# Three PSUM banks for the scores and one for the row-maximum scores, instead of two and two, in an attention and feed-forward layer

## The chip, the cores and the metric

The kernel runs on one core of one Trainium2 chip. Its metric is the device time of one launch in microseconds (us), the median of three runs: 2845.18 us before the change (2844.33 to 2846.65). The engines are named as in the profile: PE is TensorE's matmul side and PEld its loading of weights, DVE is VectorE, ACT is ScalarE, POOL is GpSimd, SP is SyncE, which here only issues DMAs. Matmuls write into PSUM, of which the kernel uses all eight banks of 512 float32 values for each of 128 partitions.

## The reference

A pre-norm layer on 16 sequences of 512 tokens and 256 channels, all float32:

```
x = x + attention(layernorm(x))      # 32 query heads over 16 key/value heads, head size 64
x = x + ffn(layernorm(x))            # rank-64 factors: U1, V1, gelu, U2, V2
scores = q @ k.T / 8 + alibi_slope * (key_pos - query_pos)   # causal, -inf above the diagonal
attn = softmax(scores);  out = (attn @ v) @ W_out
```

## The kernel before

**Splitting.** Float32 factors are split into a high and a low float16 part, and every product is the sum of three float16 matmuls. So most values pass through three engines: ACT rounds the high part out of a PSUM bank (`copy`, L677), DVE computes the low part (`low`, L836), SP moves both to the partitions at which the matmuls read them. For the softmax the order is ACT `exp` from a scores bank into `p_f` (L718), ACT `p_hi` (L677), POOL `p_lo` (L1082).

**Batches, steps, segments.** One loop iteration is one batch element `i`; it has 16 steps `s`, one for each key/value head (two query heads), and each step has 5 segments `n`. The stages run pipelined over the steps: the row maxima of head pair g stand in step g + 2, its scores and exponentials in step g + 7 (`ATT`), the product with v in the step after. With 16 batches there are 16 x 16 x 5 = 1280 blocks of scores and as many blocks of row-maximum scores. The code is written out in full for all iterations, and each engine has its own instruction stream, in the order of the code; engines wait for each other by semaphores that count finished blocks.

**Two kinds of scores.** `scores(s, n)` computes the transposed score block, keys on partitions, with the maximum already subtracted through extra rows of the operands, and ACT exponentiates it. To know the maximum beforehand, `max_scores(s, n)` computes the plain scores first (queries on partitions) and `maxima(s, n)` on DVE adds the causal mask in place in the bank and reduces it to one column (L909: one custom instruction and one reading of the accumulator for each tile; a segment has one tile of 512 columns or two of 384 + 128 or 256 + 256). After every four steps the maxima are transposed (`transpose_max`), split by ACT and DVE, and written by DMA into the query operand (`neg_max_t` to `q_hi_aug`, L388), for which PE waits at the scores of the first of the next four heads.

**PE's order within a segment** (L635 to L669): `scores(s, n)`, in some segments a feed-forward matmul or the transposition, `max_scores(s, n)`, then what the segment has of projections (k at n = 0 of odd steps, q at n = 1 of even and n = 2 of odd steps, the output projection at n = 4, v at n = 4), the attention product `attend` at n = 1 and n = 3, and the feed-forward parts. So in an even step `max_scores(s, 0)` and `max_scores(s, 1)` have only `scores(s, 1)` between them, and `max_scores(s, 2)` and `max_scores(s, 3)` only `scores(s, 3)`. In an odd step a projection stands in the first of these gaps and the q projection in the second.

**DVE's order** (L932 to L1051): in a segment first the normalised rows of the second layernorm and the low part of the transposed maxima, if due, then `maxima(s, n)`, then the low parts of v, k, q and x, the output sum (`x_acc`), and at n = 1 and n = 3 `normalise` (`rden`, `o_f`), which waits for `attend`.

**Banks and their waits.** Two banks in turn hold `scores`, two `max_scores`, one `o_acc`, three the projections and everything else. PE may write scores block b when ACT has exponentiated block b - 2, and max block b when DVE has reduced block b - 2:

```
if SEG * a + n - 1 > 0:
    pe.wait_ge(exp_done, at(SEG * a + n - 1))
bank = score_bank[(SEG * s + n) % 2]
```

Of the kernel before, what the change touches and what calls it, by code (L numbers as in the profile page):

```python
# [26 lines left out]
ACT = mybir.ActivationFunctionType  # L27
# [14 lines left out]
SEG = 5  # L42
# [51 lines left out]
def q_segment(s):  # L94

    return 2 if s % 2 else 1
# [16 lines left out]
def projection_order():  # L113

    uses = []
    for s in range(KV):
        for n in range(SEG):
            if (s, n) in H_PAIRS:
                uses += [("h", 2 * H_PAIRS[s, n]), ("h", 2 * H_PAIRS[s, n] + 1)]
            if n == MAX_SEG and s % 4 == 2:  # L120
                uses.append(("max", s))
            if (s, n) in X_PAIRS:
                uses.append(("x", X_PAIRS[s, n]))
            if n == K_SEG and s % 2 == 1:
                uses.append(("k", s))
            if n == OUT_SEG:
                uses.append(("out", s))
            if (s, n) in LN2_T_AT:
                uses.append(("ln2", LN2_T_AT[s, n]))
            if n == q_segment(s):  # L130
                uses.append(("q", s))
            if n == V_SEG and s % 8 < 4:
                uses.append(("v", s))
            if (s, n) in U1_AT:
                uses.append(("p", U1_AT[s, n]))
            if (s, n) == Y_AT:
                uses += [("y", 0), ("y", 1)]
            if (s, n) in U2_PAIRS:
                uses.append(("u", U2_PAIRS[s, n]))
    return uses  # L140

BANKS = 3
PROJ = {use: k % BANKS for k, use in enumerate(projection_order())}


# [61 lines left out]
def layer(nc, x, w_qkv, w_out, u1, v1, b1, u2, v2, b2, k_aug, q_aug, ident_d, ident_b_d, causal_d, out):  # L209
    B = x.shape[0]  # L210
    ctx = ExitStack()
    with ctx:
        def sb(name, shape, dt):
            return ctx.enter_context(nc.sbuf_tensor(name, shape, dt))

        def psum(name):
            return ctx.enter_context(nc.psum_tensor(name, [P, 512], F32))

        def sem(name):
            return ctx.enter_context(nc.semaphore(name))  # L220
# [23 lines left out]
        p_f = sb("p_f32", [P, 3, 512], F32)  # L244
# [29 lines left out]
        h_lo = sb("h_lo", [P, 2, S], F16)  # L274
        qf_hi, qf_lo = h_hi[:, 0, :], h_lo[:, 0, :]

        score_bank = [psum("scores0"), psum("scores1")]
        max_bank = [psum("max_scores0"), psum("max_scores1")]
        o_bank = psum("o_acc")
        proj_bank = [psum(f"proj{b}") for b in range(BANKS)]  # L280

# [17 lines left out]
        exp_done, hi_p, lo_p = sem("exp_done"), sem("hi_p"), sem("lo_p")  # L299
# [13 lines left out]
        block = ctx.enter_context(nc.Block())  # L313

        def at(count):

            if not isinstance(count, Count):
                return count
            if not count.regs:
                return count.value()  # L320
            if not count.plus:
                return count.regs[count.times]
            count.regs["eng"].reg_add(count.regs["target"], count.regs[count.times], count.plus)
            return count.regs["target"]

        def max_place(s, n):

            return max_bank[(SEG * s + n) % 2], 2

        def iterations(name, eng, body):  # L330
            body(Count(0), FIRST)
# [5 lines left out]
        def ffn_batch(i, s):  # L337

            return i - 1 if s >= 8 else i - 2
# [105 lines left out]
        def _(pe):  # L445
# [5 lines left out]
            def mm(out_ap, lhs, rhs, start, stop):  # L451
                return nc.tensor.matmul(out_ap, lhs, rhs, start=start, stop=stop, skip_group_check=True)  # L452
# [9 lines left out]
            def transpose_x(b, pair):  # L462

                bank = proj_bank[PROJ["x", pair]]
                if pair == 0:
                    pe.wait_ge(xn_done, at(T * (b + 1)))
                for c in range(DC):
                    for t in range(2):
                        col = (c * 2 + t) * P
                        last = nc.tensor.transpose(bank[:, col:col + P], xt[:, 2 * pair + t, c * P:(c + 1) * P], ident[:, :])  # L470
                last.then_inc(pe_ln1, 1)

            transpose_x(0, 0)
            transpose_x(0, 1)
            proj_free = {PROJ["x", pair]: (lo_ln1, pair + 1) for pair in range(2)}
            pe.wait_ge(split_done, 3)

            def body(i, mode):

                def next_proj(use, semaphore, count):  # L480

                    b = PROJ[use]
                    if b in proj_free:
# [5 lines left out]
                def scores(s, n):  # L489
                    a = i * KV + s - ATT  # L490
                    r = (s - ATT) % RING
                    if n == 0:
                        if (s - ATT) % 4 == 0:
                            q4 = (s - ATT) // 4
                            pe.wait_ge(m_in[q4 % 2], at(32 * (2 * i + q4 // 2 + 1)))

                    if SEG * a + n - 1 > 0:
                        pe.wait_ge(exp_done, at(SEG * a + n - 1))
                    bank = score_bank[(SEG * s + n) % 2]
                    for h, kt, off, width in SCORE_BLOCKS[n]:  # L500
                        keys = slice(kt * P, (kt + 1) * P)
                        o = bank[:, off:off + width]
                        mm(o, ka[:, r, keys], qa[:, r, h, kt * P:S], True, False)

                        mm(o[:, 0:P], causal[:, S - P:S], ident_b[:, :], False, False)
                        last = mm(o, kb[:, r, keys], qb[:, r, h, kt * P:S], False, True)
                    last.then_inc(pe_scores, 1)

                def max_scores(s, n):
                    g = i * KV + s - 2  # L510
                    r = (s - 2) % RING
                    if n == 0:
                        use = 2 * i + (s - 2) // RING + 1
                        pe.wait_ge(qdup_in[r], at(QK_DMAS * 16 * use))
                        if s % 2 == 0:
                            pe.wait_ge(kdup_in[r // 2], at(QK_DMAS * 16 * use))
                            pe.wait_ge(kaug_in[r // 2], at(16 * use))
                    bank, back = max_place(s, n)
                    if SEG * g + n + 1 - back > 0:
                        pe.wait_ge(max_done, at(SEG * g + n + 1 - back))  # L520
                    for h, qt, off in MAX_BLOCKS[n]:
                        width = (qt + 1) * P
                        last = mm(bank[:, off:off + width], qb[0:MAX0, r, h, qt * P:(qt + 1) * P],
                                  kb[0:MAX0, r, 0:width], True, True)
                    last.then_inc(pe_max, 1)
# [100 lines left out]
                for s in steps(mode):  # L626
# [8 lines left out]
                    for n in range(SEG):  # L635
                        if in_stage(mode, s, ATT):
                            scores(s, n)
# [37 lines left out]
        def _(act):  # L675
            def copy(out_ap, in_ap, scale=1.0):
                return nc.scalar.activation(out_ap, in_ap, ACT.Copy, scale=scale)  # L677
# [6 lines left out]
            def high_x(b, pair):  # L684
                act.wait_ge(pe_ln1, at(2 * b + pair + 1))
                copy(xnt[0][:, :, pair * 256:(pair + 1) * 256],
                     proj_bank[PROJ["x", pair]][:, :].rearrange("p (c q) -> p c q", c=DC)).then_inc(hi_ln1, 1)

# [16 lines left out]
            def body(i, mode):  # L705
                def proj(*use):
                    return proj_bank[PROJ[use]]

                def exponentiate(s, n):
                    count = SEG * (i * KV + s - ATT) + n  # L710
                    act.wait_ge(pe_scores, at(count + 1))


                    back = 2 if s == 0 and n < 2 else 3
                    if count - back + 1 > 0:
                        act.wait_ge(lo_p, at(count - back + 1))
                    k = SEG * s + n
                    nc.scalar.activation(p_f[:, k % 3, :], score_bank[k % 2][:, :], ACT.Exp).then_inc(exp_done, 1)  # L718

                def high_p(s, n):  # L720
                    a = i * KV + s - ATT
# [23 lines left out]
                for s in steps(mode):  # L745
# [3 lines left out]
                    for n in range(SEG):  # L749
# [5 lines left out]
                        if n == 0 and in_stage(mode, s, ATT + 1):  # L755
                            if s > 0:
                                high_p(s - 1, SEG - 1)
                            else:
                                a = i * KV - ATT - 1
                                act.wait_ge(exp_done, at(SEG * (a + 1)))  # L760
                                copy(p_hi[:, 1, SEG - 1, :], p_f[:, (SEG * KV - 1) % 3, :]).then_inc(hi_p, 1)
                        if in_stage(mode, s, ATT):
                            exponentiate(s, n)
# [8 lines left out]
                        if n == O_SEG and in_stage(mode, s, ATT + 1):  # L772
                            a, slot = g - ATT - 1, s % 2
# [28 lines left out]
                        if ffn_in(i, s):  # L802
                            f = ffn_batch(i, s)
# [29 lines left out]
        def _(dve):  # L833
            def low(out_ap, bank, high, scale):

                return nc.vector.scalar_tensor_tensor(out=out_ap, in0=bank, scalar=scale, in1=high,  # L836
                                                      op0=ALU.mult, op1=ALU.subtract)
# [46 lines left out]
            def low_x(b, pair):  # L884
                dve.wait_ge(hi_ln1, at(2 * b + pair + 1))
                cols = slice(pair * 256, (pair + 1) * 256)
                low(xnt[1][:, :, cols], proj_bank[PROJ["x", pair]][:, :].rearrange("p (c q) -> p c q", c=DC),
                    xnt[0][:, :, cols], 1.0).then_inc(lo_ln1, 1)
# [286 lines left out]
```

## Time and profile before

| | |
|---|---|
| median of three runs | 2845.18 us |
| the profiled execution | 2847.87 us, of which 2846.1 us span |
| PE busy | 2688.1 us, 94% |
| ACT busy | 2178.4 us, 77% |
| POOL busy | 2000.1 us, 70% |
| DVE busy | 1990.9 us, 70% |
| granted TensorE clock, mean | 0.988 |

The span is what lies between the first and the last instruction. One batch takes some 178 us. A wait in the profile is idle time of one engine just before an instruction, put down to what released it. PE and PEld are two sides of one engine: one stop of it often shows on both, so their waits are not added.

### The profile page before, as it was taken

How to read it: one execution, taken by the hardware profiler on the slowest of the kernel's cores; microseconds unless marked ns; L12 is line 12 of the kernel's file. 1: busy time of each engine (PE TensorE's matmuls, PEld its weight loads, DVE VectorE, ACT ScalarE, POOL GpSimd, SP SyncE). 2: the span in 40 equal slices, each digit the busy share in tenths (PEclk: the TensorE clock that was granted, in tenths of full speed). 3: DMA queues.
4: the chain of work that ended last, by engine and by line, in shares of the span. 5: the costliest groups of instructions: out<-in, count | busy, mean ns of one | idle time of the engine just before them, and what ended most of it. 6: DMA issues, size and time to landing. Idle time of an engine off the chain costs nothing.

```text
span 2846.1 us, 83739 instructions
## 1 busy us (share of the span) xinstructions
PE 2688.1 (94%) x31112; PEld 1835.5 (64%) x31112; DVE 1990.9 (70%) x6795; ACT 2178.4 (77%) x3892; POOL 2000.1 (70%) x1816
## 2 busy tenths in 40 slices
PE   4999999999999999999999999999999999999985
PEld 1566666666666666666666666666666666666662
DVE  6667677676766767677676777767667676777743
ACT  3777878778777887878878787787878878787782
POOL 1667777777777777777777777777767777777773
PEclk9999999999999999999999999999999999999996
DMA  6444345344444444444444445434444454445421
GB/s 169 91 97 91 87 99 93 87 96 93 95 88 96 89 91 95 87 99 96 88 95 92 94 88 101 91 87 97 89 95 94 94 87 91 96 88 101 88 45 26
DMA packets 495147, 260.83 MB, mean 92 GB/s; under 512 B 317962, under 2 KB 493066, under 8 KB 494474
## 3 DMA queue, kind: packets, MB, share of 16 engines
q1 hardware_dynamic: 494740, 255.47, 42.8%
q8 instruction: 247, 4.05, 0.6%
q14 instruction: 160, 1.31, 0.1%
HBM read 27.73 MB, written 8.39 MB: 13 GB/s over the span
## 4 chain that ended last, share of the span: by engine, by line
PE 65%; ACT 11%; issue 7%; POOL 5%; DMA 5%; SPq 4%; DVE 3%; ACTq 0%; POOLq 0%; DVEq 0%
PE proj L452 31%; PE scores L452 16%; PE o_acc L452 10%; PE max_scores L452 7%; POOL p_lo L1082 3%; ACT p_hi L677 3%; ACT p_f L718 3%; DMA o_t<-o_hi_lo 2%; ACT L718 2%; DMA q_hi_aug<-neg_max_t_lo 2%; ACT h_f L809 2%; POOL h_lo L1112 1%; POOL o_hi_lo L1094 1%; SPq L422 1%; DVE max_scores L909 1%
## 5 line engine op out<-in xcount | busy, mean ns | idle before, releaser
L1082 POOL TENSOR_TENSOR p_lo<-p_f,p_hi 128x512 f16<-128x512 f32 x1280 | 1481.5, 1169 | 778.7 <-ACT p_hi L677 777.8
L909 DVE CUSTOM_DVE_ANT_0 max_scores<-max_scores,causal 128x512 f32<-128x512 f32 (+3 forms) x2048 | 970.0, 507 | 313.7 <-PE max_scores L452 299.6
L718 ACT ACTIVATE p_f<-scores 128x512 f32<-128x512 f32 x1280 | 755.7, 590 | 169.0 <-PE scores L452 143.2
L677 ACT ACTIVATE p_hi<-p_f 128x512 f16<-128x512 f32 x1280 | 800.0, 625 | 14.2
L452 PE MATMUL scores<-q_hi_lo,k_lo_hi 128*128 128x512 f16 (+3 forms) x2048 | 614.4, 300 | 34.5 <-ACT p_f L718 18.3
L452 PE MATMUL scores<-q_hi_aug,k_hi_aug 128*128 128x512 f16 (+3 forms) x2048 | 586.1, 299 | 0.0
L452 PE MATMUL o_acc<-v_hi_one,p_lo 128*128 128x65 f16 x5120 | 517.2, 194 | 8.8 <-POOL p_lo L1082 7.8
L452 PE MATMUL max_scores<-k_hi_aug,q_hi_aug 96*128 96x512 f16 (+3 forms) x2048 | 489.8, 300 | 29.0 <-issue 17.5
L452 PE MATMUL o_acc<-v_hi_one,p_hi 128*128 128x65 f16 x5120 | 517.0, 194 | 0.0
L452 PE MATMUL o_acc<-v_lo,p_hi 128*128 128x64 f16 x5120 | 516.4, 193 | 0.0
L452 PEld LDWEIGHTS o_acc<-v_hi_one,p_lo 128*128 128x128 f16 x5120 | 471.2, 98 | 41.5 <-POOL p_lo L1082 22.8
L452 PEld LDWEIGHTS o_acc<-v_lo,p_hi 128*128 128x128 f16 x5120 | 468.1, 98 | 38.5
L452 PEld LDWEIGHTS o_acc<-v_hi_one,p_hi 128*128 128x128 f16 x5120 | 467.4, 97 | 0.0
L452 PE MATMUL scores<-ident_bf,causal 128*128 128x128 bf16 x2048 | 448.1, 219 | 0.0
L452 PE MATMUL proj<-wo_hi,o_t 128*128 128x256 f16 x2048 | 382.2, 275 | 13.7 <-DMA o_t<-o_hi_lo 13.6
L452 PE MATMUL proj<-xn_t_hi,wqkv_lo 128*128 128x512 f16 x768 | 293.6, 382 | 28.8 <-DVE x_acc L916 16.4
L1094 POOL TENSOR_TENSOR o_hi_lo<-o_f,o_hi_lo 128x512 f16<-128x512 f32 x256 | 296.3, 1157 | 3.4 <-ACT o_hi_lo L677 3.4
L452 PE MATMUL proj<-xn_t_hi,wqkv_hi 128*128 128x512 f16 x768 | 293.1, 382 | 0.0
L452 PE MATMUL proj<-xn_t_lo,wqkv_hi 128*128 128x512 f16 x768 | 293.0, 381 | 0.0
L909 DVE DVE_READ_ACCUMULATOR2_ANT row_max<- 128x1 f32 x2048 | 284.2, 139 | 1.3
L452 PE MATMUL proj<-wo_lo,o_t 128*128 128x256 f16 x1024 | 280.8, 274 | 0.0
L452 PEld LDWEIGHTS scores<-q_hi_lo,k_lo_hi 128*128 128x128 f16 x2048 | 199.6, 97 | 114.3 <-ACT p_f L718 24.8
(107 smaller groups left out, 4282.4 us busy)
## 6 DMA issues: line engine op xcount, KB each, us to landing
q_hi_aug<-q_pair_hi SPq DMA_DIRECT2D x512, 64.0 KB, 2.0
q_hi_lo<-q_pair_hi SPq DMA_DIRECT2D x512, 64.0 KB, 2.0
q_hi_lo<-q_pair_lo SPq DMA_DIRECT2D x512, 64.0 KB, 2.0
k_hi_aug<-k_pair_hi SPq DMA_DIRECT2D x256, 64.0 KB, 2.0
k_lo_hi<-k_pair_hi SPq DMA_DIRECT2D x256, 64.0 KB, 2.0
k_lo_hi<-k_pair_lo SPq DMA_DIRECT2D x256, 64.0 KB, 2.0
x_rows<-in_L_attn_inputs SPq DMA_DIRECT2D x17, 512.0 KB, 4.5
x_acc<-in_L_attn_inputs SPq DMA_DIRECT2D x64, 128.0 KB, 2.5
```

What stands on the lines that cost most here:

```text
L422: sp.dma_start_transpose(ot[:, kv % OUT_RING, :, :].rearrange("p a (t q) -> p (a t) q", q=P), o_hl[:, slot, :, :].rearrange("p a q -> p (a ...
L452: return nc.tensor.matmul(out_ap, lhs, rhs, start=start, stop=stop, skip_group_check=True)
L677: return nc.scalar.activation(out_ap, in_ap, ACT.Copy, scale=scale)
L718: nc.scalar.activation(p_f[:, k % 3, :], score_bank[k % 2][:, :], ACT.Exp).then_inc(exp_done, 1)
L809: nc.scalar.activation(h_f[:, c % 2, :], proj("h", c)[:, :], ACT.Gelu_apprx_tanh, bias=b1c[:, c:c + 1], scale=1.0 / FFN_SCALE).then_inc(ge ...
L909: last = nc.vector.tensor_tensor_reduce(out=bank, in0=bank, in1=causal[:, (T - 1 - qt) * P:S], scale=1.0, scalar=-3e38, op0=ALU.add, op1=A ...
L1082: nc.gpsimd.tensor_tensor(p_lo[:, slot, n, :], p_f[:, k % 3, :], p_hi[:, slot, n, :], ALU.subtract).then_inc(lo_p, 1)
L1094: nc.gpsimd.tensor_tensor(o_hl[:, slot, 1, :], o_f[:, slot, :, :].rearrange("p t c -> p (t c)"), o_hl[:, slot, 0, :], ALU.subtract).then_i ...
L1112: nc.gpsimd.tensor_tensor(h_lo[:, c % 2, :], h_f[:, c % 2, :], h_hi[:, c % 2, :], ALU.subtract).then_inc(lo_h, 1)
```

## The change

`scores` gets a third bank and `max_scores` keeps one, so that eight banks remain in use. PE may now write scores block b when ACT has exponentiated block b - 3, and max block b when DVE has reduced block b - 1. Nothing else is edited.

```diff
 BANKS = 3
+SCORE_BANKS = 3
 PROJ = {use: k % BANKS for k, use in enumerate(projection_order())}
...
-        score_bank = [psum("scores0"), psum("scores1")]
-        max_bank = [psum("max_scores0"), psum("max_scores1")]
+        score_bank = [psum(f"scores{b}") for b in range(SCORE_BANKS)]
+        max_bank = psum("max_scores")
...
         def max_place(s, n):
 
-            return max_bank[(SEG * s + n) % 2], 2
+            return max_bank, 1
...
-                    if SEG * a + n - 1 > 0:
-                        pe.wait_ge(exp_done, at(SEG * a + n - 1))
-                    bank = score_bank[(SEG * s + n) % 2]
+                    block = (SEG * a + n).value()
+                    if block - SCORE_BANKS + 1 > 0:
+                        pe.wait_ge(exp_done, block - SCORE_BANKS + 1)
+                    bank = score_bank[block % SCORE_BANKS]
...
-                    nc.scalar.activation(p_f[:, k % 3, :], score_bank[k % 2][:, :], ACT.Exp).then_inc(exp_done, 1)
+                    nc.scalar.activation(p_f[:, k % 3, :], score_bank[count.value() % SCORE_BANKS][:, :], ACT.Exp).then_inc(exp_done, 1)
```

Both programs have the same instructions in the same order on every engine; bank names and the counts that PE waits for differ. PE, segments 0 and 1 of an even step, before:

```order
9300 L452 MATMUL scores0<-q_hi_lo,k_lo_hi 128x512 [waits exp_done]
9301 L452 MATMUL scores0<-ident_bf16,causal 128x128
9302 L452 MATMUL scores0<-q_hi_aug,k_hi_aug 128x512
9303 L452 MATMUL max_scores0<-k_hi_aug,q_hi_aug 128x512 [waits kaug_in2,max_done,kdup_in2,qdup_in4]
9304 L452 MATMUL scores1<-q_hi_lo,k_lo_hi 128x512 [waits exp_done]
9305 L452 MATMUL scores1<-ident_bf16,causal 128x128
9306 L452 MATMUL scores1<-q_hi_aug,k_hi_aug 128x512
9307 L452 MATMUL max_scores1<-k_hi_aug,q_hi_aug 128x384 [waits max_done]
9308 L452 MATMUL max_scores1<-k_hi_aug,q_hi_aug 128x128
```

The same place of PE in the changed kernel:

```order
9300 L453 MATMUL scores2<-q_hi_lo,k_lo_hi 128x512 [waits exp_done]
9301 L453 MATMUL scores2<-ident_bf16,causal 128x128
9302 L453 MATMUL scores2<-q_hi_aug,k_hi_aug 128x512
9303 L453 MATMUL max_scores<-k_hi_aug,q_hi_aug 128x512 [waits kaug_in2,max_done,kdup_in2,qdup_in4]
9304 L453 MATMUL scores0<-q_hi_lo,k_lo_hi 128x512 [waits exp_done]
9305 L453 MATMUL scores0<-ident_bf16,causal 128x128
9306 L453 MATMUL scores0<-q_hi_aug,k_hi_aug 128x512
9307 L453 MATMUL max_scores<-k_hi_aug,q_hi_aug 128x384 [waits max_done]
9308 L453 MATMUL max_scores<-k_hi_aug,q_hi_aug 128x128
```

Nothing moved. Row 9307 waited for the maxima of the block before 9303 and now waits for those of 9303 itself, which stands four matmuls ahead of it; row 9304 waits for an exponential that lies one block further back.

## Rows read from the trace of the kernel before

**Rows 1.** The page, section 1: busy time of each engine.
```profile
PE 2688.1 (94%) x31112; PEld 1835.5 (64%) x31112; DVE 1990.9 (70%) x6795; ACT 2178.4 (77%) x3892; POOL 2000.1 (70%) x1816
```

**Rows 2.** Waits of PEld: engine, line, releaser: total us, times, longest us.
```profile
PEld scores L452 <- ACT p_f L718: 24.8, 52, 2.7
PEld scores L452 <- DMA q_hi_aug<-neg_max_t_lo: 24.7, 26, 1.9
PEld o_acc L452 <- POOL p_lo L1082: 22.8, 51, 2.2
PEld proj L452 <- DVE k_pair_lo L836: 20.1, 64, 2.3
PEld max_scores L452 <- DVE row_max L909: 16.9, 25, 1.8
```

**Rows 3.** Timeline, PEld, step 14: start us, us, ..., loads for max blocks 0, 1, 3.
```profile
990.87 0.10 PEld L452 LDWEIGHTS max_scores<-k_hi_aug,q_hi_aug 96*128 96x128 f16 x1
991.58 0.10 PEld L452 LDWEIGHTS max_scores<-k_hi_aug,q_hi_aug 96*128 96x128 f16 x1
...
995.92 0.10 PEld L452 LDWEIGHTS max_scores<-k_hi_aug,q_hi_aug 96*128 96x128 f16 x1
```

**Rows 4.** Timeline, PE: matmuls of max block 1, in step 14 and in step 0.
```profile
991.79 0.38 PE L452 MATMUL max_scores<-k_hi_aug,q_hi_aug 96*128 96x384 f16 x2
...
842.62 0.39 PE L452 MATMUL max_scores<-k_hi_aug,q_hi_aug 96*128 96x384 f16 x2
```

**Rows 5.** Timeline, DVE, step 14: maxima of block 0, then around block 2.
```profile
991.64 0.70 DVE L909 CUSTOM_DVE_ANT_0 max_scores<-max_scores,causal 128x512 f32<-128x512 f32 x1 [0.38 <-issue]
992.26 0.14 DVE L909 DVE_READ_ACCUMULATOR2_ANT row_max<- 128x1 f32 x1
...
996.08 0.28 DVE L836 SCALAR_TENSOR_TENSOR neg_max_t_lo<-proj,neg_max_t_hi 32x128 f16<-32x128 f32 x1 [0.61 <-ACT neg_max_t_hi L677]
996.28 0.41 DVE L909 CUSTOM_DVE_ANT_0 max_scores<-max_scores,causal 128x256 f32<-128x256 f32 x1
...
997.01 0.13 DVE L909 DVE_READ_ACCUMULATOR2_ANT row_max<- 128x1 f32 x1
```

**Rows 6.** Timeline, PEld, step 4: loads for max blocks 0, 1, 3.
```profile
889.00 0.10 PEld L452 LDWEIGHTS max_scores<-k_hi_aug,q_hi_aug 96*128 96x128 f16 x1
...
889.71 0.31 PEld L452 LDWEIGHTS max_scores<-k_hi_aug,q_hi_aug 96*128 96x128 f16 x2
...
893.60 0.10 PEld L452 LDWEIGHTS max_scores<-k_hi_aug,q_hi_aug 96*128 96x128 f16 x1
```

**Rows 7.** Timeline, DVE, step 4: before and in block 0, then block 2's last reading.
```profile
889.56 0.69 DVE L836 SCALAR_TENSOR_TENSOR v_lo<-proj,v_hi_one 128x512 f16<-128x512 f32 x1 [1.73 <-ACT v_hi_one L677]
890.17 0.41 DVE L916 SCALAR_TENSOR_TENSOR x_acc<-proj,x_acc 128x256 f32<-128x256 f32 x1
...
891.10 0.14 DVE L909 DVE_READ_ACCUMULATOR2_ANT row_max<- 128x1 f32 x1
...
894.19 0.14 DVE L909 DVE_READ_ACCUMULATOR2_ANT row_max<- 128x1 f32 x1
```

**Rows 8.** Step 0: PEld's two stops; DVE's last readings before block 0 and in it.
```profile
842.62 0.11 PEld L452 LDWEIGHTS max_scores<-k_hi_aug,q_hi_aug 96*128 96x128 f16 x2 [0.47 <-DVE row_max L909]
844.17 0.10 PEld L452 LDWEIGHTS proj<-xn_t_hi,wqkv_lo 128*128 128x128 f16 x1 [1.44 <-DVE xn_t_lo L836]
...
842.42 0.14 DVE L909 DVE_READ_ACCUMULATOR2_ANT row_max<- 128x1 f32 x1
...
844.57 0.14 DVE L909 DVE_READ_ACCUMULATOR2_ANT row_max<- 128x1 f32 x1
```

**Rows 9.** Step 11: PEld's load for max block 3, DVE's end of block 2.
```profile
965.33 0.10 PEld L452 LDWEIGHTS max_scores<-k_hi_aug,q_hi_aug 96*128 96x128 f16 x1
...
965.95 0.14 DVE L909 DVE_READ_ACCUMULATOR2_ANT row_max<- 128x1 f32 x1
```

**Rows 10.** The tile `max_scores`: all its weight loads, first and last start.
```profile
L452 PEld LDWEIGHTS max_scores<-k_hi_aug,q_hi_aug x2048: 95/98/152, 44.4 to 2734.5; 96*128 96x128 f16 x187
```

**Rows 11.** Stretches: length, busy of PE, PEld, DVE, ACT, POOL, granted clock, DMA, GB/s.
```profile
1178.00:2600.00 1422.00, 1385.16 (x16216) 953.89 (x16213) 1020.67 (x3522) 1133.22 (x2030) 1038.88 (x943) 1.00 0.44 92
...
2730.00:2740.00 10.00, 6.59 (x102) 5.15 (x100) 4.38 (x17) 9.37 (x16) 7.92 (x8) 1.00 0.15 29
```

## The prediction

> **What bounds the kernel now.** I read the busy times first: PE has 94%, the next engine 77% [rows 1], and in the long steady stretch PE is busy for 1385 of 1422 us [rows 11]. PE works through its list in order, so a stop of PE anywhere, once the pipeline is full, is time added to the end unless a later stop that is there already shrinks by it. Then the waits of PEld, where PE's stops begin [rows 2]. The two that the change touches are small: 24.8 us behind ACT's exponential, 16.9 us behind DVE's maxima. The third view is the timeline of PE and DVE around the max blocks [rows 3 to 9]. It decides, because the change swaps two distances: PE may run three scores blocks ahead of ACT instead of two, and one max block ahead of DVE instead of two, so that writing a max block and reading it no longer overlap at all.
>
> **What the third scores bank removes.** The wait for `p_f` [rows 2], at most 24.8 us. With the block three back to wait for, which ACT has done a whole segment earlier, I expect all 52 stops to go, and then PE comes earlier to the next max block, where part is lost again. I take 20 us; the ends are 0 and 24.8.
>
> **What the single max bank adds.** PE's new rule: the matmuls of max block b start when DVE's last accumulator reading of block b - 1 has ended, plus the signal. The signal can be read where PE waited for just that: DVE's reading ended at 842.42 + 0.14 = 842.56, the load came at 842.62 [rows 8], so 0.06 us, and the matmul began with it [rows 4]. Where PE does not wait, a matmul can start up to 0.21 us after its load (991.58 and 991.79) [rows 3, 4], as the array is still busy. So I count delays by the matmuls: load start plus 0.21 at n = 1, plus 0.06 at n = 3, where the matmul ahead is narrow.
>
> Even steps, n = 1 (only one scores block between the two max blocks). Step 14: DVE ends block 0 at 992.26 + 0.14 = 992.40 [rows 5], PE could start at 992.46 and had started at 991.79 [rows 4]: 0.67 us. DVE began that block only 0.77 us after PE's load of it (990.87 to 991.64) and works 0.76 us, so the loop of PE, DVE and back is 1.59 us, where the loads are 0.71 us apart; a stop of PE before it shifts all of it and shortens nothing. I take 0.70 us for the five steps 6 to 14. In steps 2 and 4 DVE comes to the block later, behind `v_lo`, which waited for ACT and through it for PE's own v projection, and `x_acc`: end 891.10 + 0.14, start possible at 891.30, was 889.71 + 0.21 = 889.92: 1.38 us [rows 6, 7].
>
> Even steps, n = 3. Step 4: block 2 ends at 894.33, so 894.39 against 893.66: 0.73 [rows 6, 7]; I take 0.75 for steps 0, 4, 8, 12, since DVE has the h of the second layernorm in front in one of them. In steps 2, 6, 10, 14 DVE waits for ACT's transposed maxima before block 2 and ends at 997.14: 997.20 against 995.98, 1.22 us [rows 3, 5].
>
> Step 0 has two stops already, and what counts is when the q projection starts: 844.17 before [rows 8]. After, max block 1 can start at 844.57 + 0.14 + 0.06 = 844.77 and its two matmuls take 0.39 us to their modelled end [rows 4], of which the next overlaps the larger part: I take 0.22, so 844.99: 0.8 us more.
>
> Odd steps are mostly free, since a projection stands between. The exceptions are step 11 at n = 3, behind a long `h_f` on DVE: 965.95 + 0.14 + 0.06 = 966.15 against 965.39, 0.76 us [rows 9]; and step 5, where the feed-forward end crowds DVE in the same manner (estimate 0.8), and small ones, estimated from the same pattern at 0.8 together.
>
> Per batch: 5 x 0.70 + 2 x 1.38 + 4 x 0.75 + 4 x 1.22 + 0.8 + 2.4 = 3.5 + 2.8 + 3.0 + 4.9 + 0.8 + 2.4 = 17.4 us. Sixteen batches: 278 us.
>
> **What of it is hidden.** A stop hides in a later stop of PE whose releaser was started before the first. (1) PE waits for the DMA of the transposed maxima, 24.7 us [rows 2]. Its chain starts at n = 2 of steps 6, 10, 14, 2, ahead of the 1.22 us stop at n = 3, and the wait follows at the next step's n = 0. 24.7 / 26 = 0.95 us, mostly below 1.22: I take 16 of the 24.7. (2) PE waits for `p_lo`, 22.8 us: the last exponential lies before n = 1 of the step, so the n = 1 stop lies partly in between: half, 11 us. (3) PE waits for `k_pair_lo`, 20.1 us: in odd steps, right behind its own projection, which shifts with PE: 0. (4) The maxima wait, 16.9 us, mostly at step 0, is inside the 0.8 there. The ends are 0 and the whole of (1) to (3), 67.6 us.
>
> **Sum.** 278 - 20 - 16 - 11 = 231 us on the profiled execution's 2847.9 us: 3079 us. That execution is 2.7 us above the median of the runs, so 3076 us. ACT, POOL and DVE have room for nothing worse: their busy shares fall to some 71, 65 and 65%, and they are waited for less than before.
>
> **Rivals.**
> 1. *PE's other waits swallow more.* All of the removable and hidden ones go in full: 278 - 24.8 - 67.6 = 186 us, 3031 us after the 2.7. For it: ACT and POOL get 8% more time for the same work. Against: the k wait hangs on PE itself.
> 2. *DVE never catches up.* The price of a stop above assumes that DVE works off its backlog while PE stands, so that the second stop of a step is not larger for the first. If every late finish counts in full: of the 1280 blocks (the first and last of their 2048 loads at 44.4 and 2734.5 [rows 10]) I find 433 whose load started before DVE had ended the block ahead, 390 us in sum and 416 us with the signal. 416 - 25 = 391 us, 3236 us. Against: in step 14 DVE idled 0.38 us before block 0 [rows 5], so it starts each even step without backlog, and a stop counted by its load is 0.15 us too long at n = 1.
> 3. *The clock.* The new stops, about 16 in a batch, take PE from 97% to some 90% busy. If TensorE's granted clock fell from 1.00 to a mean of 0.95, 5% of PE's 2688 us come on top, 134 us: 3210 us. Against: in 2730 to 2740 us PE was busy for 6.6 of 10 us with stops like these and was granted 1.00 [rows 11].
> 4. *Not slower.* The waits do not bind, because DVE's reading fits between the blocks, and only the third scores bank shows: 2847.9 - 24.8 = 2823 us, 2820 after the 2.7. It decides at n = 1 of the even steps: DVE would have to end 0.06 us before 991.79. It works 0.76 us by itself, from 991.64 on, which is longer than the whole 0.71 us between the loads. Nothing in the trace speaks for it but the small total of the present wait (16.9 us), which says only that two blocks of distance were enough.
>
> The Trainium skill bears on rival 3: its page "TensorE: Matmul & The Clock Gate", section "A second HAM failure mode: psum-queue depth-cycling", tells of a kernel whose matmul groups of 512 columns cycled through PSUM banks with short idle times between them, and whose clock swung between the two levels. By that rule this change, which makes just such pauses, would end at rival 3's time or above. The row at 2730 us disagrees, and it stands at 4%.
>
> **Chances.** Forecast (3040 to 3130) 0.70; rival 1 (3000 to 3040) 0.15; rival 2 (above 3130) 0.09; rival 3 0.04; rival 4 0.02. The likeliest is 3076 us. The range for 8 in 10 is 3015 to 3145. What a measurement can tell from no change is about 0.2%, 5.7 us; only rival 4 leads to faster (0.01) or the same (0.01), slower has 0.98.
>
> **What would show it.** In the changed profile PEld's wait for `row_max` rises from 16.9 to some 250 to 300 us with about 300 stops, at n = 1 and n = 3 of even steps. A stop's next load comes 0.06 us after DVE's reading. The wait for `p_f` is gone. The wait for the maxima's DMA shrinks to less than half. The granted clock stays at 0.98 or more. PE's busy time hardly moves, its share falls to 87%. I am wrong if the stops stand elsewhere, or if their sum is right and the time is not because other waits grew: ACT's exponential behind POOL, or `o_acc` behind `p_lo`.

## The result, and the profile after

The changed kernel takes 3095.5 us, the median of four runs (3093.2 to 3096.3), against 2845.9 us, the median of four runs of the kernel before: a ratio of 1.0875, 95% interval 1.0856 to 1.0894. It is 250 us slower. Forecast were 3076 us and 3015 to 3145. The profiled execution took 3095.6 us.

The page after: busy time of the engines (section 1), which answers to [rows 1]. PE has the same matmuls and 89% of the span instead of 94%; DVE, ACT and POOL have lost share as well. So nothing became a bottleneck by its work, and PE stands still more: its idle time grew by 197 us and its busy time, which was to stay as it was with a share of 87%, by 51 us.

```profile
PE 2738.7 (89%) x31112; PEld 1838.0 (59%) x31112; DVE 2059.5 (67%) x6795; ACT 2178.3 (70%) x3892; POOL 2006.3 (65%) x1816
```

PEld's waits after, as in [rows 2] (a line number is one or two higher where the new lines shift it):

```profile
PEld max_scores L453 <- DVE row_max L911: 324.2, 301, 3.2
PEld proj L453 <- issue: 60.2, 136, 9.7
PEld max_scores L453 <- issue: 57.6, 64, 2.5
PEld proj L453 <- DVE k_pair_lo L838: 18.9, 64, 2.1
...
PEld o_acc L453 <- POOL p_lo L1084: 12.2, 9, 3.4
...
PEld scores L453 <- ACT p_f L720: 1.8, 2, 1.0
...
PEld scores L453 <- DMA q_hi_aug<-neg_max_t_lo: 0.7, 3, 0.3
```

Read against [rows 2]: the wait for DVE's maxima went from 16.9 us in 25 stops to 324.2 us in 301; the wait for the exponential, from 24.8 to 1.8; for the maxima's DMA, from 24.7 to 0.7; for `p_lo`, from 22.8 to 12.2; for `k_pair_lo` it stayed (20.1 and 18.9). A wait of PEld is up to 0.2 us longer than what the matmuls lose, so 324 us of waits are not 324 us of time. The row for the maxima also leaves some out: of the 64 stops put down to `issue`, 30, with 30.6 us, stand before block 0 of a step and end 0.12 us after DVE's last reading of the block before, so they are waits for the maxima too. PE has a further semaphore instruction there, since block 0 also waits for the DMAs of q and k, and the profile names no releaser for them.

The timeline after, PEld and then DVE, step 14 of one batch: start us, duration us, instruction, and in brackets the idle time before it and its releaser. It is the place of [rows 3, 5].

```profile
1084.18 0.10 PEld L453 LDWEIGHTS max_scores<-k_hi_aug,q_hi_aug 96*128 96x128 f16 x1 [0.69 <-issue]
...
1085.58 0.11 PEld L453 LDWEIGHTS max_scores<-k_hi_aug,q_hi_aug 96*128 96x128 f16 x2 [0.83 <-DVE row_max L911]
...
1090.65 0.10 PEld L453 LDWEIGHTS max_scores<-k_hi_aug,q_hi_aug 96*128 96x128 f16 x1 [1.22 <-DVE row_max L911]
```

```profile
1083.93 0.14 DVE L911 DVE_READ_ACCUMULATOR2_ANT row_max<- 128x1 f32 x1
...
1084.77 0.70 DVE L911 CUSTOM_DVE_ANT_0 max_scores<-max_scores,causal 128x512 f32<-128x512 f32 x1 [0.42 <-issue]
1085.38 0.14 DVE L911 DVE_READ_ACCUMULATOR2_ANT row_max<- 128x1 f32 x1
...
1090.46 0.13 DVE L911 DVE_READ_ACCUMULATOR2_ANT row_max<- 128x1 f32 x1
```

PE and DVE take turns. DVE's reading of block 0 ends at 1085.52 and PE's load of block 1 comes at 1085.58; the reading of block 2 ends at 1090.59 and the load of block 3 comes at 1090.65. Both are the 0.06 us forecast, and the second stop, 1.22 us, is the number of the prediction. The first load here shows something new: block 0 itself waited 0.69 us. It is one of the 30 stops without a releaser: DVE's last reading of the block before, block 4 of step 13, ends at 1084.07, and the load comes at 1084.18.

Step 4 after, the place of [rows 6, 7], PEld and then DVE:

```profile
974.27 0.11 PEld L453 LDWEIGHTS max_scores<-k_hi_aug,q_hi_aug 96*128 96x128 f16 x2 [1.55 <-DVE row_max L911]
```

```profile
972.53 0.69 DVE L838 SCALAR_TENSOR_TENSOR v_lo<-proj,v_hi_one 128x512 f16<-128x512 f32 x1 [1.25 <-ACT v_hi_one L679]
973.14 0.41 DVE L918 SCALAR_TENSOR_TENSOR x_acc<-proj,x_acc 128x256 f32<-128x256 f32 x1
...
974.07 0.14 DVE L911 DVE_READ_ACCUMULATOR2_ANT row_max<- 128x1 f32 x1
```

`v_lo` and `x_acc` still stand ahead of block 0 on DVE, and PE now waits for the end of that row of work.

Stretches after (length, busy of PE, PEld, DVE, ACT, POOL, granted clock, DMA share, GB/s), which answer to [rows 11]:

```profile
0.00:160.00 160.00, 100.05 (x750) 51.24 (x751) 94.86 (x266) 70.06 (x113) 50.94 (x44) 0.87 0.44 112
...
1000.00:1194.00 194.00, 176.58 (x2055) 120.09 (x2053) 133.85 (x449) 142.10 (x256) 131.25 (x120) 1.00 0.42 87
1194.00:2800.00 1606.00, 1460.89 (x16826) 989.58 (x16825) 1098.51 (x3661) 1172.68 (x2104) 1079.27 (x980) 1.00 0.41 85
```

PE is busy for 91% of the steady stretch, at a granted clock that rounds to 1.00.

### The profile page after: what moved, and what is told of

The parts are those of the page before. It is cut to its first block and busy times, and to the rows that moved or that the text cites. A ratio compares the mean times of both kernels' runs of the same rounds, so it can differ in the third digit from the quotient of the medians.

```text
span 3093.8 us, 83739 instructions
## 1 busy us (share of the span) xinstructions
PE 2738.7 (89%) x31112; PEld 1838.0 (59%) x31112; DVE 2059.5 (67%) x6795; ACT 2178.3 (70%) x3892; POOL 2006.3 (65%) x1816
## 3 DMA queue, kind: packets, MB, share of 16 engines
q14 instruction: 160, 1.31, 0.1%
## 5 line engine op out<-in xcount | busy, mean ns | idle before, releaser
L453 PE MATMUL max_scores<-k_hi_aug,q_hi_aug 96*128 96x512 f16 (+3 forms) x2048 | 496.4, 303 | 286.6 <-DVE row_max L911 268.8
L453 PEld LDWEIGHTS o_acc<-v_hi_one,p_lo 128*128 128x128 f16 x5120 | 474.1, 98 | 36.7 <-POOL p_lo L1084 12.2
L453 PEld LDWEIGHTS max_scores<-k_hi_aug,q_hi_aug 96*128 96x128 f16 x2048 | 181.3, 98 | 408.2 <-DVE row_max L911 324.2
L679 ACT ACTIVATE q_pair_hi<-proj 128x512 f16<-128x512 f32 x256 | 152.5, 596 | 248.2 <-PE proj L453 248.2
```

## The experiments

Each ran beside the kernel before, which took 2849.9 to 2851.1 us there. The changed kernel itself was measured beside a kernel before of 2845.9 us; by its ratio of 1.0875 it is set at 3100.5 us in these comparisons. The intervals of two ratios leave such a difference uncertain by some 7 us.

**Without the third scores bank**

```diff
-SCORE_BANKS = 3
+SCORE_BANKS = 2
```

> Two scores banks in turn and one max bank (seven banks in use): the changed kernel without its third scores bank. Theory (the single max bank costs, the third scores bank gives a little back): the stops of PE before the scores in segment 4 of steps 1, 3 and 13 return, 1.33 us per batch by the comparison of the two traces, so 3096 + 21 = 3117 us, within 3108 to 3125. Rival (the third bank is worth nothing once PE waits for maxima, since ACT has caught up during those waits): 3096 us within 5.

Measured: 3105.1 us, ratio 1.0899 (1.0881 to 1.0918), so 4.6 us above the changed kernel's 3100.5; the two profiles' last max blocks lie 10.8 us apart. The intervals overlap. The time lies below the expected range of 3108 to 3125 us, and the rival, within 5 us of the changed kernel, is nearer: the third bank is worth 5 to 11 us, not 21. Its PEld waits for the exponential and for the maxima:

```profile
PEld max_scores L453 <- DVE row_max L911: 323.3, 300, 3.2
...
PEld scores L453 <- ACT p_f L720: 22.5, 45, 2.7
```

The stops before the scores came back as expected, but not in the time. Block by block, the two traces part by 0.49 us at segment 4 of step 1, 0.40 us in step 3 and 0.46 us in step 13, and come together again by 0.47 us at block 0 of step 14. There the changed kernel has the 0.69 us stop seen above. Block 0 of step 14 waits for two things, DVE's maxima of the block before and the DMAs of k's low part. SP had issued two of these (timeline of the changed kernel, SP's issues), the second 0.6 us behind the first, at 1081.56, and such a DMA lands 2.0 us after its issue (the page, section 6: KB each, us to landing):

```profile
1080.93 1.23 SPq L406 DMA_DIRECT2D k_lo_hi<-k_pair_lo  x2
```

```profile
k_lo_hi<-k_pair_lo SPq DMA_DIRECT2D x256, 64.0 KB, 2.0
```

So k was there at 1083.56, 0.6 us before the load, and it was DVE's reading, which ended at 1084.07, that held PE. Over the batches, 9 of the 16 stops end 0.12 us after DVE's last reading, with k landed 0.1 to 0.8 us before the load; in six the load comes 0.06 us after k's last landing, and for one the trace shows no cause. In the run with two banks stops of both kinds are 0.3 to 0.5 us shorter: the third bank brings PE there some 0.5 us earlier, but not DVE or k. So what the third bank wins in step 13 PE spends at step 14, in most batches waiting for DVE's maxima, else for k. The places, sizes and times are measured; no run removed either wait.

**Only the wait, no shared bank**

```diff
-            return max_bank[(SEG * s + n) % 2], 2
+            return max_bank[(SEG * s + n) % 2], 1
```

> The kernel before with its two banks of each kind in turn, and only the count in the wait of the max blocks tightened: block b waits for the maxima of block b - 1. No bank is shared between a matmul being written and a block being read. Theory (the loss is the wait itself, PE writing and DVE reading in series): the same as the run with two scores banks and one max bank, about 3117 us, within 3 us of that run. Rival (part of the loss is that PE and DVE meet in the same bank, a slower access or restart): clearly below that run, by 10 us or more.

Measured: 3109.7 us, ratio 1.0910 (1.0894 to 1.0926), 4.6 us above the run before, with 324.4 us in 301 waits for DVE's maxima. That is more than the 3 us expected, the intervals overlap, and of the 6 us between the two profiles 3.4 lie at step 0, where the clock fell in six batches instead of four (see the last part). Two banks in turn do not help once the wait is tightened, and the rival, 10 us or more below, is out. The loss is the order in time, PE writes, DVE reads, PE writes; that both use the same PSUM bank costs nothing that shows.

**The q projection between max blocks 0 and 1**

```diff
-                        if in_stage(mode, s, 2):
+                        if in_stage(mode, s, 2) and not (n == 1 and s % 2 == 0):
                             max_scores(s, n)
...
                             project(next_proj(("q", s), lo_q, i * KV + s + 1), s * P, pe_q)
+                        if in_stage(mode, s, 2) and n == 1 and s % 2 == 0:
+                            max_scores(s, n)
```

> The changed kernel, and in even steps max_scores(s, 1) is written after the q projection of its segment instead of ahead of it, which puts 1.3 us of matmuls between max blocks 0 and 1 and takes them from between blocks 1 and 2. Theory (stops come from max blocks that lie closer on PE than the 1.5 to 1.6 us of writing, reading and signalling): the stops of five steps (0.69 us by matmuls) go and those of steps 2 and 4 shrink by 1.2 us, block 2 stays free: 16 x (3.45 + 2.4) = 94 us less, 3002 us, within 2985 to 3025. Rival (DVE is too slow on the whole, and a stop that is avoided at block 1 comes back at block 2 or 3): 3080 to 3100 us, with stops of 0.7 us or more at n = 2.

Measured: 2976.5 us, ratio 1.0444 (1.0428 to 1.0460): 124 us less, where 94 were expected. Waits for the maxima fell to 188.1 us in 210. No stop came back at block 2. I had left out step 0 (1.0 us per batch) and taken too little for steps 2 and 4; with the next stops of steps 10 and 12 (0.18 and 0.36 us less) the two traces part by 121 us in all. The rival, a DVE too slow on the whole, falls: with the same work for DVE half of the loss is gone.

**A shorter reading of block 0**

```diff
-                        bank = max_place(s, n)[0][:, off:off + (qt + 1) * P]
+                        width = 2 * P if n == 0 else (qt + 1) * P
+                        bank = max_place(s, n)[0][:, off + (qt + 1) * P - width:off + (qt + 1) * P]
...
-                            out=bank, in0=bank, in1=causal[:, (T - 1 - qt) * P:S], scale=1.0, scalar=-3e38,
+                            out=bank, in0=bank, in1=causal[:, S - width:S], scale=1.0, scalar=-3e38,
```

> The changed kernel, but DVE takes the maximum of block 0 of every step over its last 256 columns instead of all 512 (that part of the computation is left out), so this reading is shorter by some 0.26 us (0.75 us against 0.49 us for a first tile of 256 columns in the trace), and nothing is moved. Theory (DVE's reading stands on PE's path at n = 1 of the eight even steps, one to one): 8 x 0.26 x 16 = 33 us less, 3063 us, within 3055 to 3070. Rival (the stops are set by when DVE comes to the block, by ACT or by its backlog, and the length of one reading is absorbed): under 10 us less, 3086 to 3096 us.

Measured: 3067.1 us, ratio 1.0762 (1.0746 to 1.0778): 33 us less, as the theory has it, and 29 us less by the two profiles; the intervals do not tell the two apart. Block 1's load comes 0.25 to 0.27 us earlier in seven of the eight even steps, 0.20 in step 8. Two later stops grew, (10, 3) and (12, 3) (step, segment) by 0.23 and 0.25 us, 8 us in sum, since there DVE was held by the second layernorm and not by PE. A microsecond saved on DVE in front of a waiting PE is one on PE, unless the next stop hangs on something that did not move.

**The low part of v behind the maxima**

```diff
-    return 1 if s >= 8 else 0
+    return 1
```

> The changed kernel, and DVE computes the low part of v always after the next step's maxima of block 0 instead of ahead of them, as it does already for the second half of the heads. Theory (in steps 2 and 4 the stop of PE at max block 1 is 1.4 us instead of 0.7 because v_lo and x_acc stand ahead of block 0 on DVE): these two stops shrink by the 0.6 us of v_lo each, 2 x 0.6 x 16 = 19 us less than the changed kernel. Rival (the projection bank that v_lo frees later makes PE wait elsewhere, or the stop is held by x_acc anyway): within 6 us of the changed kernel.

Measured: 3074.7 us, ratio 1.0779 (1.0760 to 1.0798): 26 us less, 19 expected. The waits at block 1 of steps 2 and 4 fell from 1.54 and 1.65 us to 0.88 and 0.89, the size of those of steps 6 to 14, with `x_acc` still ahead of block 0. So their excess was `v_lo`, and not `x_acc`.

**Max block 3 behind the attention product, in addition** (`MAX_AFTER` names the steps' segments whose max block is written later, and behind what)

```diff
+MAX_AFTER = {(0, 1): 'q', (0, 3): 'attend'}      # (s % 2, n)
...
+                def max_at(s, n, place):
+                    if in_stage(mode, s, 2) and MAX_AFTER.get((s % 2, n), "segment") == place:
+                        max_scores(s, n)
...
                             attend(s, n // 2)
+                        max_at(s, n, "attend")
```

> As the run with the q projection ahead of max block 1, and in even steps max block 3 is written after the attention product of its segment (0.92 us more distance from block 2, 0.92 us less to block 4). Theory (each stop is 1.5 to 1.6 us minus the distance on PE): at n = 3 the four plain stops go (0.75 us each) and the four behind the transposed maxima shrink by 0.92, 107 us; at n = 4 steps 6, 8, 10, 12 have only 0.7 us left and get stops of some 0.8 us, 54 us: 53 us less than that run, 2923 us, within 2900 to 2945. Rival (DVE as a whole is late by then, its backlog decides): no gain, 2960 to 2985.

Measured: 2917.1 us, ratio 1.0222 (1.0207 to 1.0238), 60 us below the run with q ahead of block 1; 53 expected. Waits for the maxima fell to 120.6 us. At n = 4 new waits stand where they were expected: 0.86, 0.68, 0.47 and 0.47 us in steps 6, 8, 10 and 12.

**All max blocks spread**

```diff
+MAX_AFTER = {(0, 0): 'scores1', (0, 1): 'q', (0, 3): 'attend', (0, 4): 'out',
+             (1, 0): 'k', (1, 1): 'attend', (1, 2): 'q', (1, 3): 'attend', (1, 4): 'out'}
```

> The changed kernel with the max blocks spread evenly over PE's list: block 0 of even steps after scores block 1, all others at the end of their segment, after the projection, attention product or output projection in it, so that no two stand closer than about 1.5 us. Theory (distance decides): the stops shrink to those at step 0 and behind the transposed maxima and the second layernorm, some 2 us per batch; with the third scores bank this is 2850 to 2885 us. Rival (DVE's other work, q, k, v low parts and the normalisation, now comes too late behind the maxima, and new waits of PE for them replace the old ones): 2900 us or more, with stops of PE before o_acc or the projections.

Measured: 2961.0 us, ratio 1.0377 (1.0362 to 1.0393), where 2850 to 2885 were expected. The rival won: 44 us worse than the run before. PEld's waits in this run, the two longest:

```profile
PEld proj L454 <- DVE k_pair_lo L848: 84.4, 64, 2.3
PEld max_scores L454 <- DVE row_max L921: 77.7, 197, 2.1
```

The waits for the maxima shrank as intended, and the wait for the low part of k grew from 19 to 84 us. DVE works in order with the maxima first in each segment, so a max block that PE writes late holds back `k_pair_lo`, whose bank PE needs for the next projection. With the odd steps as they were, two runs further down, this wait is back at 19.1 us.

**The same order with two and two banks**

> The same spread order with the banks of the kernel before, two for the scores and two for the maxima. Theory (with two max banks DVE had slack enough, so the order is worth nothing by itself): within 10 us of the kernel before. It also says what single bank costs once the blocks are spread: the theory expects under 35 us between this run and the spread run with three and one. Rival (the spread order delays DVE's other results): 20 us or more slower than the kernel before.

Measured: 2921.9 us, ratio 1.0244 (1.0229 to 1.0259), 71 us above the kernel before, where at most 10 were expected: the rival again, and with the same wait:

```profile
PEld proj L453 <- DVE k_pair_lo L846: 85.4, 64, 3.1
```

So most of the loss of the spread order is its own, and the banks add 39 us to it, a little over the 35 that were allowed.

**Spread in the even steps alone**

```diff
+MAX_AFTER = {}
+MAX_AFTER.update({(s, 1): 'q' for s in range(0, 16, 2)})
+MAX_AFTER.update({(s, 3): 'attend' for s in range(0, 16, 2)})
+MAX_AFTER.update({(s, 4): 'out' for s in (6, 8, 10, 12)})
...
-    return 1 if s >= 8 else 0
+    return 1
```

> Three scores banks and one max bank; max block 1 of even steps after the q projection, block 3 of even steps after the attention product, block 4 of steps 6, 8, 10 and 12 after the output projection, v_lo late as in the run with the low part of v; odd steps as in the kernel before, since the fully spread order made PE wait 84 us for the low part of k. Theory (distance on PE against 1.5 to 1.6 us): from the run with max block 3 after the attention product the stops at n = 4 of the four steps go, (0.86 + 0.68 + 0.47 + 0.47) x 16 = 40 us, of which some 6 us come back at block 0 of step 7, and v_lo gives 14 us: 2917 - 48 = 2869 us, within 2855 to 2890. Rival (new waits for other low parts, as in the fully spread order): 2900 us or more.

Measured: 2893.3 us, ratio 1.0158 (1.0140 to 1.0177). By the ratios that is 18 us below the run with block 3 behind the attention product, and 48 were expected: a miss. The waits at n = 4 are gone, and `row_max` is down to 67.3 us, but block 0 of steps 7 and 13 now waits 0.63 and 0.50 us, which stands in the row of `issue`:

```profile
PEld max_scores L457 <- issue: 69.5, 90, 2.2
PEld max_scores L457 <- DVE row_max L924: 67.3, 123, 1.6
```

Of the 69.5 us in the first row, 47.0 us in 58 stops end 0.12 us after DVE's last reading, so they are waits for the maxima as well; in the changed kernel these were 30.6 us. I had counted only step 7 behind its moved block, and not step 13. By the two traces steps 6 to 13 gave 12 us, where 40 less 6 were expected, and `v_lo` gave 4 us for 14, since with block 1 behind the q projection the stops of steps 2 and 4 were already down to 0.40 and 0.50 us. It is the best order found for three and one banks, and it does not reach the kernel before.

**That order with two and one, and with two and two banks**

> The same order, with two scores banks and one max bank. Theory (the third scores bank was worth only 7 us in the changed kernel because the stops before max blocks repay it at steps 14, 2 and 4; with fewer such stops it is worth more): 12 to 25 us slower than the same order with three scores banks. Rival (its worth does not depend on them): 5 to 9 us slower.

> The same order, with two banks of each kind as in the kernel before. Theory (with two max banks the order matters little): within 10 us of the kernel before, and 15 to 30 us faster than the same order with two scores banks and one max bank, since some 100 us of stops before max blocks become about 20 us and other waits of PE take a part of the difference. Rival (the order itself costs): 15 us or more slower than the kernel before.

Measured: 2904.6 us with two and one, ratio 1.0199 (1.0178 to 1.0220), and 2853.6 us with two and two, ratio 1.0017 (1.0008 to 1.0027). The third scores bank is worth 11 us here, just under the 12 to 25 of the theory and above the rival's 9; the intervals of the two ratios touch, so that it is worth more than in the changed kernel stays open. The reason that the theory gave does not hold at step 14: at its block 0 PE still gives back 0.55 us per batch. The order by itself is nearly free, 0.17% slower than the kernel before. The second max bank is worth 51 us even in this order, where 15 to 30 were expected: to bring the blocks apart removed 80% of the loss with two and one banks (255 us, now 51) and not all of it. With three and one banks, the banks of the change, 40 us are left.

## Why the prediction was right

The mechanism was right, place by place, and the time is 20 us above the likeliest value, a miss of 8% of the change. The two traces, compared at the first matmul of each max block and averaged over the batches, give for each of the prediction's terms (us per batch):

| term | predicted | measured |
|---|---|---|
| n = 1, steps 6 to 14 (five) | 3.5 | 3.67 |
| n = 1, steps 2 and 4 | 2.8 | 2.81 |
| n = 3, steps 0, 4, 8, 12 | 3.0 | 3.51 |
| n = 3, steps 2, 6, 10, 14 | 4.9 | 5.09 |
| step 0, beyond its old stops | 0.8 | 1.31 |
| steps 5 and 11, and small ones | 2.4 | 1.43 |
| added, in sum | 17.4 | 17.8 |
| third scores bank | -1.25 | -1.34 |
| of it spent again at step 14 | not in the sum | +0.44 |
| the maxima's DMA, now hidden | -1.0 | -1.09 |
| `p_lo` and the rest | -0.7 | -0.36 |
| sum | 14.4 | 15.5 |
| times 16 | 231 us | 248 us |

**The sum of the stops** was forecast at 278 us and is 285. Steps 2 and 4 (the run with v's low part), the length of the reading (the run with the shorter one) and the distance (the run with q between) were each confirmed by a run. The largest miss of a place is n = 3 of step 12, 1.29 us where I took 0.75: I had named the second layernorm's `h_f` in front of DVE and not priced it, though [rows 9] price the same thing in step 11. The small stops of the odd steps, estimated at 0.8 us, are not there. At step 0 the 0.8 us were right: nine batches measure 0.84 each. Block 0 itself stops there for 1.24 us, which the prediction did not name, but the old stop of the q projection takes that up. In five batches the clock fell and step 0 cost 1.6 us more, and this makes the mean 1.31. So the sum is as near as it is partly by luck: 16 us too much for the odd steps stand against 8 us for the clock and 11 us too little at n = 3.

**The third scores bank**: all but 2 of 52 stops went, as forecast. The prediction took 20 us as what is left of 24.8 after a part is lost again at the next max block. The table has 21 us before the loss and 14 after it, and the two-and-one run gives 5 to 11 us. So the kind was right, a stop at the next max block, block 0 of step 14, which in most batches waits for DVE's maxima; the size of what is lost again was taken too small, 5 us where the traces show 7 to 12.

**What is hidden**: the DMA of the maxima gave 17 us for the 16 taken (its wait on PEld fell by 24.0 us, and the matmuls behind it came 1.09 us a batch closer, 0.78 of it at step 7). For `p_lo` 11 us were taken: its wait fell by 10.6 us, but step 14, where 14 of its 51 waits stood, came only 0.19 us a batch closer, 3 us, and the other places are not to be told from the rest. No run tried either.

**The rivals.** The first needed 92 us to be removed or hidden, the third bank's gain included, and it was 38 (2.35 x 16). The second, stops that grow because DVE does not catch up, is out by 140 us: the n = 3 stops are not larger for the n = 1 stops ahead of them (0.73 to 0.75 us in steps 0, 4 and 8, where 0.73 was read off), and with q between the blocks no stop came back at block 2. One reason given against it was too wide: in steps 0, 2 and 4 DVE does come to block 0 late. The fourth is out by 275 us. The third, the clock, was wrong in size and not wholly in kind, as the next part but one shows.

## What to carry to other kernels

Before a double buffer is given up, look in the timeline for the closest pair of its blocks on the writer, and set write + signal + read + signal against that distance: here 1.59 us against 0.71 us, at two places in each second step, while the total of the waits for that buffer (16.9 us) and every engine's busy share said nothing of it. A buffer whose waits are short is not one that is not needed. And a stop that the profile puts down to `issue` can be a wait all the same: set its end against the last instruction of the engine that it may wait for. If the bank has to go, move the writer's other work between the close pair, and only there: an even spread delayed the reader's other results, and cost 71 us by itself.

## What the runs showed of the hardware that was not expected

TensorE's clock fell in the steady part of the changed kernel, which the rounded 1.00 of the long stretches hides. Short stretches of the changed kernel around step 0 of one batch, columns as above:

```profile
550.00:554.00 4.00, 1.87 (x12) 0.83 (x11) 3.45 (x11) 3.50 (x7) 2.99 (x4) 1.00 0.37 82
554.00:558.00 4.00, 4.00 (x36) 2.29 (x37) 0.87 (x4) 1.55 (x3) 2.19 (x2) 0.57 0.34 66
558.00:562.00 4.00, 3.43 (x58) 2.49 (x54) 3.28 (x11) 2.50 (x5) 2.99 (x3) 1.00 0.36 80
```

PE was busy for 1.87 us of 4, as its two stops of step 0 follow each other, and in the next 4 us the granted clock was 0.57, which is 3.4 of them at 1.2 GHz instead of 2.4. A projection matmul of 512 columns shows the difference on PE, once at the one level and once at the other:

```profile
554.24 0.63 PE L453 MATMUL proj<-xn_t_hi,wqkv_lo 128*128 128x512 f16 x1
...
1085.81 0.38 PE L453 MATMUL proj<-xn_t_hi,wqkv_lo 128*128 128x512 f16 x1
```

The Trainium skill ("TensorE: Matmul & The Clock Gate", "A second HAM failure mode: psum-queue depth-cycling") tells of a kernel whose clock swung between the two levels because TensorE idled briefly and often between groups of matmuls. In this trace that has a small part: the clock fell where two stops crowd, and not at single stops of 1.2 us, which stand in every second step at 1.00. Between 160 and 2980 us there are five such falls, each right behind the stops of step 0 of a batch, and the kernel before has none between 160 and 2750 us. In ten other batches the same two stops left the clock at 1.00, so they do not always bring it down. A fall cost about 1.6 us, all five 8 us. In the first 160 us, while the pipeline fills, the granted clock was 0.87, in the kernel before 0.95, and the changed kernel is 24 us behind after the first 70 max blocks, where the later batches add some 15 each: it may be the clock there too, which no run separated.

The signal from DVE's last instruction to PE's next load took 0.05 to 0.06 us in each of the 301 stops, and 0.12 us in the 30 before a block 0, where PE executes one more semaphore instruction. A matmul behind a stop starts with its load (both at 1085.58 in step 14), not 0.2 us later as in a full stream. So a stop costs the matmul stream up to 0.2 us less than the wait that the profile shows for the load.
